# The last steps of an attention block: where PE transposes the normalised rows and VectorE takes their extremes

## The chip, the cores and the metric

The kernel runs on one core of one Trainium2 chip. The metric is the device time of the program in microseconds, from one launch. The engines are named as in the profile: PE is TensorE, DVE is VectorE, ACT is ScalarE, POOL is GpSimd, and SP is the engine whose queue issues all the DMAs here.

## The reference, cut to what matters

Eight batches of 128 rows of 512 pass through cross attention (32 query heads of 128, 4 heads of keys and values, 256 keys from the context and from the rows themselves) and through a feed-forward block whose activations are quantised by their largest and smallest value over all batches.

```python
x = x + xattn(_layernorm(x), ctx_4096, Wq, Wk, Wv, Wo)
x = x + ffn(_layernorm(x), w_gate, w_up, w_down)

def act_qdq(x, bits=16):                 # used on the input of the ffn first
    mn = jnp.minimum(jnp.min(x), 0.0)    # over the whole tensor
    mx = jnp.maximum(jnp.max(x), 0.0)
    scale = jnp.maximum((mx - mn) / qmax, 1e-12)
    ...
```

So between the two halves stands a layer norm of every batch and an extreme over all eight.

## The kernel before, in words

Attention is cut into 64 steps (`STEPS`), 16 for each of the four key heads (`QUADS`): step t takes batch `t % 16 // 2` and four of the eight query heads of that key head. The last 16 steps, 48 to 63, finish the batches, two steps for each. All operands are split in two fp16 parts, a high one written by ACT and a low one by DVE.

Each engine runs one loop over t with its own list written out by hand; engines meet at semaphores alone, and each works strictly in its order.

- PE (from line 463): `scores(t + 2)`, `project(t - 1)` (the heads times Wo, into `y`), `q_first(t + 6)`, `head_out(t)` (probabilities times values), `q_second(t + 6)`. There is no more q after step 57, and no more scores after step 61. In steps 60 to 63 `transpose_x2(b)` turns the rows of batches 0 to 6 into banks for the feed-forward block, four transposes a batch, by the table `X2_AT`; before the change it stands ahead of `project(t - 1)`. It waits for the rows (`ln2_out`) and, from batch 2, for the copy of the batch two before (`x2_copied`).
- ACT: `p_upper(t + 1)`, `exps(t + 2)`, `copy_x2(b)` by the same table, the high part of the head's output (`o_hi`), `q_upper(t + 6)`. `exps` waits for `maxima` (`max_out`).
- DVE: `maxima(t + 2)`, `p_lower(t + 1)`, work on the feed-forward weights (`unit_scales`, `unit_round`, `unit_lo`), in even steps `add_y(t - 1)`, `reciprocals(t + 2)`, in even steps from 50 `ln2_stats(b)`, the low part of the head's output (`o_lo`), `q_lower(t + 6)`, and in even steps from 50 `ln2_apply(b)`, with b = `t % 16 // 2 - 1`. `ln2_apply` waits for the root from POOL (`ln2_rstd`), writes the normalised rows (`xln2`), then takes the largest and smallest of each row of `y` (`y_extremes`) and scales them into `stats`.
- POOL: `unit_normalise`, `unit_dequantise`, `normalise(t + 2)` (four operations, one for each head, waiting for the reciprocals), and in even steps from 50 `ln2_root(b)`.
- SP: `turn_p(t + 1)`, a DMA that transposes the probabilities of the next step as soon as `p_lower` has written them, and around it the loads and stores of weights; in steps 49 to 59 also two transposing loads of ready weights after each turn (line 263).

After the loop come the last projection, 12 matmuls that only keep PE busy, the transposes of batch 7, and a short chain of small operations that gives the quantiser of the feed-forward input; then ACT and DVE round the input and PE starts on the gate.

Lines in the profile: 413 is `scores`, 423 `head_out`, 437 and 441 `project`, 450 `transpose_x2`, 323 the q matmuls (a helper), 499 gate and up, 350 the warming matmuls; 798 and 801 are `maxima`, 809 `reciprocals`, 852 the rows, 837, 838 and 857 the extremes and their statistic, 842 to 846 `ln2_stats`, 864 `add_y`; 743 is every low part (with 1024 columns it is `p_lower`), 558 every high part (with 1024 columns `p_upper`), 600 the exps, 611 `copy_x2`; 1112 is `normalise`, 1136 and 1142 are units, 1146 is `ln2_root`; 259 is `turn_p`.

Of the kernel before, what the change touches and what calls it, by code (L numbers as in the profile page):

```python
# [19 lines left out]
B, T, H = 8, 128, 512  # L20
# [6 lines left out]
QUADS = 16  # L27
# [23 lines left out]
P_FIRST = 8  # L51
OQ_PIECES = [(0, 0, 2), (0, 2, 5), (0, 5, FT)] + [(b, *span) for b in range(1, B) for span in ((0, 5), (5, FT))]
X2_AT = {60: (0, 1), 61: (2, 3), 62: (4, 5), 63: (6,)}
EARLY = 4
SLOT_OF = (5, 9, 13, 25)
WO_AT = (1, 2, 3, 4, 5, 6, 13, 14)
# [3 lines left out]
def units_at(t, stage):  # L60

    n = t - stage
    return (EARLY + n // 2,) if n >= 0 and n % 2 == 0 and EARLY + n // 2 < UNITS else ()

# [19 lines left out]
def build(nc, x, ctx_t, wq, wk, wv, wo, w_units, w_ready, out):  # L84
    stack = ExitStack()
    with stack:
# [11 lines left out]
        def sem(name):  # L98
            return stack.enter_context(nc.semaphore(name))
# [102 lines left out]
        ln2_stat, ln2_mv, ln2_var, ln2_rstd, ln2_out = (sem(n) for n in ("ln2_stat", "ln2_mv", "ln2_var", "ln2_rstd", "ln2_out"))  # L202
# [114 lines left out]
        def _(pe):  # L317
# [63 lines left out]
            def q_head(f, i):  # L381

                h, pair = 2 * (f % 4) + i, f % QUADS // 4
                return three(banks[QB + f % 2][:, i * 256:i * 256 + 256],
                             lambda r, c: wq_s[:, r, c, h * D:(h + 1) * D],
                             lambda r, c: src_t[:, 5, r, c, pair * 256:(pair + 1) * 256], HC)
# [9 lines left out]
            def q_second(f):  # L396

                q_head(f, 1).then_inc(q_mm, 1)
# [28 lines left out]
            def project(t):  # L427

                par, hq = t // QUADS % 2, t % 2
                if t % QUADS == 0:  # L430
                    pe.wait_ge(wo_lo, t // QUADS * GH + GH)
                if hq == 0 and t >= 2:
                    pe.wait_ge(y_add, t // 2)
                pe.wait_ge(o_hi, t + 1)
                for hh in range(4):
                    for r in range(2):
                        nc.tensor.matmul(banks[YB][:, :], o_s[:, 0, hh * P:(hh + 1) * P], wo_s[:, par, r, hq * 4 + hh, :],  # L437
                                         start=hq == 0 and hh == 0 and r == 0, stop=False)
                pe.wait_ge(o_lo, t + 1)
                for hh in range(4):  # L440
                    mm = nc.tensor.matmul(banks[YB][:, :], o_s[:, 1, hh * P:(hh + 1) * P], wo_s[:, par, 0, hq * 4 + hh, :],  # L441
                                          start=False, stop=hq == 1 and hh == 3)
                mm.then_inc(wo_mm, 1)

            def transpose_x2(b):
                pe.wait_ge(ln2_out, b + 1)
                if b >= 2:
                    pe.wait_ge(x2_copied, b - 1)
                for c in range(HC):
                    mm = nc.tensor.transpose(banks[QB + b % 2][:, c * P:(c + 1) * P], xln2[:, b, c * P:(c + 1) * P], ident[:, :])  # L450
                mm.then_inc(x2_mm, 1)
# [19 lines left out]
            for t in range(STEPS):  # L471
                f = t + Q_AHEAD
                if t + AHEAD < STEPS:
                    scores(t + AHEAD)
                for b in X2_AT.get(t, ()):
                    transpose_x2(b)
                if t >= 1:
                    project(t - 1)
                if f < STEPS:
                    q_first(f)  # L480
                head_out(t)
                if f < STEPS:
                    q_second(f)
            project(STEPS - 1)
            keep_warm(12)
            transpose_x2(B - 1)
# [69 lines left out]
        def _(act):  # L556
            def hi(dst, src, scale):
                return nc.scalar.activation(dst, src, ACT.Copy, scale=scale)  # L558
# [29 lines left out]
            def q_upper(f):  # L588
                act.wait_ge(q_mm, f + 1)
                head = 2 * (f % 4)  # L590
                hi(q_s[:, f // 4 % 2, 0, head:head + 2, :], banks[QB + f % 2][:, :].rearrange("p (h t) -> p h t", h=2),
                   PROJ_OUT).then_inc(q_hi, 1)
# [16 lines left out]
            def copy_x2(b):  # L609
                act.wait_ge(x2_mm, b + 1)  # L610
                nc.scalar.activation(x2t[:, :, b * P:(b + 1) * P], banks[QB + b % 2][:, :].rearrange("p (c t) -> p c t", c=HC),
                                     ACT.Copy, scale=1.0).then_inc(x2_copied, 1)
# [40 lines left out]
            for t in range(STEPS):  # L653
                f = t + Q_AHEAD
                if t + 1 < STEPS:
                    p_upper(t + 1)
                for v in units_at(t, 2):
                    unit_hi(v)
                for n in wo_at(t):
                    wo_upper(n)  # L660
                if t + AHEAD < STEPS:
                    exps(t + AHEAD)
                for b in X2_AT.get(t, ()):
                    copy_x2(b)
                act.wait_ge(pv_mm, t + 1)
                if t >= 1:
                    act.wait_ge(wo_mm, t)
                hi(o_s[:, 0, :], banks[OB][:, :], HEAD_OUT).then_inc(o_hi, 1)
                if f < STEPS:
                    q_upper(f)  # L670
            copy_x2(B - 1)

            def rounded(dst, src, q):
# [66 lines left out]
        def _(dve):  # L740
# [62 lines left out]
            def p_lower(t):  # L803
                dve.wait_ge(p_hi, t + 1)
                lo(p_16[:, t % 2, 1, :], p_s[:, t % 2].rearrange("p c h t -> p (c h t)"), p_16[:, t % 2, 0, :], 1.0).then_inc(p_lo, 1)
# [30 lines left out]
            def y_extremes(b):  # L836
                nc.vector.tensor_reduce(y_ext[:, b, 0:1], y[:, b, :], AX.X, ALU.max)
                nc.vector.tensor_reduce(y_ext[:, b, 1:2], y[:, b, :], AX.X, ALU.min).then_inc(y_ext_out, 1)

            def ln2_stats(b):  # L840
                dve.wait_ge(y_add, (NG - 1) * B + b + 1)
                nc.vector.bn_stats(bn[:, b, :], y[:, b, :]).then_inc(ln2_stat, 1)
                dve.wait_ge(ln2_stat, b + 1)
                nc.vector.bn_aggr(mv[:, b, :], bn[:, b, :]).then_inc(ln2_mv, 1)
                dve.wait_ge(ln2_mv, b + 1)
                nc.vector.tensor_scalar(veps[:, b:b + 1], mv[:, b, 1:2], 1e-5, None, ALU.add).then_inc(ln2_var, 1)
                if b == B - 1:
                    y_extremes(b)

            def ln2_apply(b):  # L850
                dve.wait_ge(ln2_rstd, b + 1)
                nc.vector.tensor_scalar(xln2[:, b, :], y[:, b, :], mv[:, b, 0:1], rstd[:, b:b + 1], ALU.subtract, ALU.mult).then_inc(ln2_out, 1)
                if b < B - 1:
                    y_extremes(b)

                dve.wait_ge(y_ext_out, b + 1)
                nc.vector.tensor_scalar(stats[:, QX, :, b], y_ext[:, b, :], mv[:, b, 0:1], rstd[:, b:b + 1],
                                        ALU.subtract, ALU.mult).then_inc(x2_stat, 1)
# [65 lines left out]
            for t in range(STEPS):  # L924
                f = t + Q_AHEAD
                final = t >= STEPS - QUADS
                if t + AHEAD < STEPS:
                    maxima(t + AHEAD)
                if t + 1 < STEPS:
                    p_lower(t + 1)  # L930
                for v in units_at(t, 0):
                    unit_scales(v)
                for v in units_at(t, 1):
                    unit_round(v)
                for v in units_at(t, 3):
                    unit_lo(v)
                for n in wo_at(t):
                    wo_lower(n)
                if t >= 2 and t % 2 == 0:
                    add_y(t - 1)  # L940
                if t + AHEAD < STEPS:
                    reciprocals(t + AHEAD)
                for n in wq_at(t):
                    wq_lower(n)
                if final and t % QUADS >= 2 and t % 2 == 0:
                    ln2_stats(t % QUADS // 2 - 1)
                dve.wait_ge(o_hi, t + 1)
                lo(o_s[:, 1, :], banks[OB][:, :], o_s[:, 0, :], HEAD_OUT).then_inc(o_lo, 1)
                if f < STEPS:
                    q_lower(f)  # L950
                if final and t % QUADS >= 2 and t % 2 == 0:
                    ln2_apply(t % QUADS // 2 - 1)
            nc.vector.memset(ones, 1.0).then_inc(ones_set, 1)
            add_y(STEPS - 1)
            ln2_stats(B - 1)
            ln2_apply(B - 1)


# [129 lines left out]
            for i in range(len(OQ_PIECES) + 4):  # L1088
                if i < len(OQ_PIECES):
                    b, first, end = OQ_PIECES[i]  # L1090
# [127 lines left out]
```

## Time and profile before

| what | value |
|---|---|
| time, median of 3 runs | 842.85 us (842.85, 842.87, 840.63) |
| time of the profiled execution | 840.5 us, its span 838.7 us |
| mean granted TensorE clock | 0.979 |
| PE busy | 780.6 us, 93% |
| DVE busy | 600.7 us, 72% |
| ACT busy | 435.4 us, 52% |
| POOL busy | 229.7 us, 27% |

The span runs from the first to the last instruction; all times of rows are microseconds from its start. Attention ends at about 615 us. The shares are means over stages with different limits, so that what an edit in steps 50 to 63 is worth has to be read in their own stretch.

### The profile page before, as it was taken

Reading aid. Unit: us, or ns where it says so; the run is one execution under the profiler, and the core shown is the slowest. Engines: PE = TensorE matmul, PEld = TensorE weight load, DVE = VectorE, ACT = ScalarE, POOL = GpSimd, SP = SyncE. Lnnn points to the kernel's source line nnn. Section 1 sums busy time; section 2 is a strip of 40 time slices with the busy share of each in tenths; the row PEclk is TensorE's granted clock in tenths of the full one; section 3 lists DMA queues with packets and bytes.
Section 4 is the critical chain, followed back from the end, with each engine's and each line's share of the span. In section 5 each row is a group of like instructions: output and inputs, shape, how many; then the busy total and the mean of one; then the engine's idle time right before and its main releaser. Section 6 shows DMA issues by size and latency. Waiting matters only on the chain.

```text
span 838.7 us, 12575 instructions
## 1 busy us (share of the span) xinstructions
PE 780.6 (93%) x4747; PEld 464.9 (55%) x4747; DVE 600.7 (72%) x1110; ACT 435.4 (52%) x946; POOL 229.7 (27%) x366
## 2 busy tenths in 40 slices
PE   8998999999999999999999999998779999931998
PEld 3455566666666666666666666665334444410443
DVE  5874558778767778767778768998746459979431
ACT  6253456655656655655655655554532019763910
POOL 0210303456443355443356343442200000000000
PEclk9999999999999999999999999999999999975999
DMA  9221055866555666455666446987651000000010
GB/s 320 69 76 51 15 144 114 181 141 137 114 127 117 172 150 132 110 126 125 164 151 141 102 99 138 170 179 137 128 109 35 1 0 1 1 1 0 26 38 38
DMA packets 203436, 85.49 MB, mean 102 GB/s; under 512 B 170352, under 2 KB 186736, under 8 KB 203376
## 3 DMA queue, kind: packets, MB, share of 16 engines
q1 hardware_dynamic: 203376, 84.69, 44.1%
q8 instruction: 37, 0.61, 0.3%
q14 instruction: 23, 0.19, 0.1%
HBM read 31.72 MB, written 10.75 MB: 51 GB/s over the span
## 4 chain that ended last, share of the span: by engine, by line
PE 78%; DVE 9%; DMA 3%; POOL 3%; ACT 3%; issue 3%; SPq 1%; ACTq 0%; POOLq 0%; DVEq 0%
PE bank L323 22%; PE bank L499 14%; PE bank L437 11%; PE bank L413 8%; PE bank L423 8%; PE bank L550 7%; PE bank L441 6%; POOL arena L1112 2%; DMA arena<-in_x 2%; DVE arena L743 2%; ACT arena L675 1%; DVE arena L1073 1%; DMA arena<-in_w_units 1%; ACT arena L600 1%; DVE nraw L798 1%
## 5 line engine op out<-in xcount | busy, mean ns | idle before, releaser
L323 PE MATMUL bank<-arena 128*128 128x256 f16 (+1 forms) x1872 | 261.0, 292 | 4.9 <-DVE arena L743 3.4
L323 PEld LDWEIGHTS bank<-arena 128*128 128x128 f16 x1872 | 182.8, 98 | 87.0 <-DVE arena L743 5.4
L1112 POOL TENSOR_SCALAR arena<-arena,rsum 128x256 f32<-128x256 f32 x256 | 132.7, 518 | 311.6 <-DVE rsum L809 297.4
L743 DVE SCALAR_TENSOR_TENSOR arena<-bank,arena 128x512 f16<-128x512 f32 x168 | 114.6, 688 | 118.1 <-ACT arena L558 117.9
L743 DVE SCALAR_TENSOR_TENSOR arena<-arena 128x512 f16<-128x512 f32 (+5 forms) x196 | 171.0, 885 | 26.4 <-ACT arena L558 26.4
L558 ACT ACTIVATE arena<-bank 128x512 f16<-128x512 f32 x168 | 98.7, 598 | 168.1 <-PE bank L423 92.5
L558 ACT ACTIVATE arena<-arena 128x512 f16<-128x512 f32 (+6 forms) x172 | 135.2, 809 | 43.5 <-POOL arena L1112 18.6
L600 ACT ACTIVATE arena<-bank,nmax 128x256 f32<-128x256 f32 x256 | 117.6, 471 | 60.5 <-DVE nmax L801 60.5
L437 PE MATMUL bank<-arena 128*128 128x512 f16 x512 | 121.0, 379 | 1.3 <-ACT arena L558 1.2
L499 PE MATMUL bank<-arena 128*128 128x512 f16 x528 | 115.8, 383 | 2.1 <-DVE arena L743 2.1
L413 PE MATMUL bank<-arena 128*128 128x256 f16 x768 | 94.3, 273 | 2.8 <-DVE arena L743 2.8
L423 PE MATMUL bank<-arena 128*128 128x512 f16 x384 | 93.4, 379 | 3.0 <-DMA arena<-arena 3.0
L499 PEld LDWEIGHTS bank<-arena 128*128 128x128 f16 x528 | 52.0, 99 | 65.9 <-issue 4.8
L413 PEld LDWEIGHTS bank<-arena 128*128 128x128 f16 x768 | 75.0, 98 | 12.7 <-DVE arena L743 3.4
L798 DVE TENSOR_REDUCE nraw<-bank 128x4 f32<-128x1024 f32 x64 | 78.3, 1223 | 3.2 <-PE bank L413 3.2
L437 PEld LDWEIGHTS bank<-arena 128*128 128x128 f16 x512 | 49.8, 98 | 49.0 <-ACT arena L558 1.5
L675 ACT ACTIVATE arena<-arena,qc 128x1024 int32<-128x1024 f32 (+5 forms) x58 | 60.4, 1080 | 28.3 <-DVE qc L981 28.3
L441 PE MATMUL bank<-arena 128*128 128x512 f16 x256 | 65.7, 379 | 0.0
L423 PEld LDWEIGHTS bank<-arena 128*128 128x128 f16 x384 | 37.2, 98 | 36.9 <-DMA arena<-arena 4.9
L550 PE MATMUL bank<-arena 128*128 128x512 f16 x264 | 57.1, 379 | 0.0
L600 ACT ACTIVATION_READ_ACCUMULATOR arena<-bank,nmax 128x1 f32 x256 | 51.8, 202 | 0.0
L1013 DVE TENSOR_SCALAR_CACHE_REDUCE arena<-bank 128x512 f32<-128x512 f32 x44 | 30.2, 687 | 26.1 <-PE bank L499 26.0
(93 smaller groups left out, 482.6 us busy)
## 6 DMA issues: line engine op xcount, KB each, us to landing
arena<-in_w_units SPq DMA_DIRECT2D x33, 256.0 KB, 3.6
w_ready<-arena SPq DMA_DIRECT2D x33, 256.0 KB, 3.3
arena<-in_wq SPq DMA_DIRECT2D x32, 256.0 KB, 3.5
arena<-in_wo SPq DMA_DIRECT2D x32, 256.0 KB, 3.6
arena<-in_x SPq DMA_DIRECT2D x1, 2048.0 KB, 15.3
out<-arena SPq DMA_DIRECT2D x8, 256.0 KB, 2.0
arena<-in_wk SPq DMA_DIRECT2D x4, 256.0 KB, 4.6
arena<-in_ctx_t SPq DMA_DIRECT2D x4, 256.0 KB, 5.0
```

What stands on the lines that cost most here:

```text
L323: last = nc.tensor.matmul(bank, a(i, c), b(j, c), start=start and c == 0 and n == 0, stop=stop and c == chunks - 1 and n == 2)
L413: mm = nc.tensor.matmul(o, q_s[:, buf, i, h, (b % 2) * P:(b % 2) * P + P], kv5[:, g + 1, r, :, b * P:(b + 1) * P], start=n == 0, stop=n == 2)
L423: mm = nc.tensor.matmul(banks[OB][:, :], kv[:, g + 1, 2 + i, (c * B + b) * P:(c * B + b + 1) * P], pt_s[:, t % 2, r, c, :], start=c == 0 a ...
L437: nc.tensor.matmul(banks[YB][:, :], o_s[:, 0, hh * P:(hh + 1) * P], wo_s[:, par, r, hq * 4 + hh, :], start=hq == 0 and hh == 0 and r == 0, ...
L441: mm = nc.tensor.matmul(banks[YB][:, :], o_s[:, 1, hh * P:(hh + 1) * P], wo_s[:, par, 0, hq * 4 + hh, :], start=False, stop=hq == 1 and hh ...
L499: mm = nc.tensor.matmul(banks[bank][:, :], wgu[:, m * FT + t, i, c * P:(c + 1) * P], xq[:, j, c, th * 512:(th + 1) * 512], start=c == 0 an ...
L550: mm = nc.tensor.matmul(banks[b % 4][:, :], oq[:, h, t, b * P:(b + 1) * P], wd_s[:, t, r, :], start=t == 0 and m == 0, stop=t == FT - 1 an ...
L558: return nc.scalar.activation(dst, src, ACT.Copy, scale=scale)
L600: nc.scalar.activation(p_s[:, t % 2, :, hh, :], bank[:, (hh % 2) * 256:(hh % 2) * 256 + 256].rearrange("p (c t) -> p c t", c=2), ACT.Exp, ...
L743: return nc.vector.scalar_tensor_tensor(out=dst, in0=src, scalar=scale, in1=part, op0=ALU.mult, op1=ALU.subtract)
L798: nc.vector.tensor_reduce(nraw[:, :], psum[:, s:s + 2, :].rearrange("p b (h t) -> p (b h) t", h=2), AX.X, ALU.max, negate=True).then_inc(n ...
L1112: done = nc.gpsimd.tensor_scalar(p_s[:, t % 2, :, hh, :], p_s[:, t % 2, :, hh, :], rsum[:, t % 2, hh:hh + 1], P_SCALE, ALU.mult, ALU.mult)
```

## The change

Four edits. On PE `transpose_x2` moves from between `scores` and `project` to the end of the step; on ACT `copy_x2` moves from ahead of the head's copy to the end of the step. On DVE the normalised rows of batch b move from the end of an even step to the next odd step, behind `p_lower` (steps 51, 53, ..., 63). The extremes are taken out of `ln2_apply` and `ln2_stats` into `ln2_extremes`, and follow the table `EXT_AT`: batches 0 to 3 at the end of that same odd step, batches 4, 5 and 6 at the end of steps 61, 62 and 63. After the loop batch 7's extremes and statistic come ahead of its rows.

```diff
+EXT_AT = {51: 0, 53: 1, 55: 2, 57: 3, 61: 4, 62: 5, 63: 6}
...
@@ PE, the loop over steps
                 if t + AHEAD < STEPS:
                     scores(t + AHEAD)
-                for b in X2_AT.get(t, ()):
-                    transpose_x2(b)
                 if t >= 1:
                     project(t - 1)
...
                 if f < STEPS:
                     q_second(f)
+                for b in X2_AT.get(t, ()):
+                    transpose_x2(b)
@@ ACT, the loop over steps
                     exps(t + AHEAD)
-                for b in X2_AT.get(t, ()):
-                    copy_x2(b)
                 act.wait_ge(pv_mm, t + 1)
...
                 if f < STEPS:
                     q_upper(f)
+                for b in X2_AT.get(t, ()):
+                    copy_x2(b)
@@ DVE, ln2_stats, ln2_apply
-                if b == B - 1:
-                    y_extremes(b)

             def ln2_apply(b):
                 dve.wait_ge(ln2_rstd, b + 1)
                 nc.vector.tensor_scalar(xln2[:, b, :], y[:, b, :], mv[:, b, 0:1], rstd[:, b:b + 1], ALU.subtract, ALU.mult).then_inc(ln2_out, 1)
-                if b < B - 1:
-                    y_extremes(b)
-
+
+            def ln2_extremes(b):
+                y_extremes(b)
+                dve.wait_ge(ln2_rstd, b + 1)
                 dve.wait_ge(y_ext_out, b + 1)
                 nc.vector.tensor_scalar(stats[:, QX, :, b], y_ext[:, b, :], mv[:, b, 0:1], rstd[:, b:b + 1],
                                         ALU.subtract, ALU.mult).then_inc(x2_stat, 1)
@@ DVE, the loop over steps
                 if t + 1 < STEPS:
                     p_lower(t + 1)
+                if final and t % QUADS >= 3 and t % 2 == 1:
+                    ln2_apply(t % QUADS // 2 - 1)
...
                     q_lower(f)
-                if final and t % QUADS >= 2 and t % 2 == 0:
-                    ln2_apply(t % QUADS // 2 - 1)
+                if t in EXT_AT:
+                    ln2_extremes(EXT_AT[t])
             nc.vector.memset(ones, 1.0).then_inc(ones_set, 1)
             add_y(STEPS - 1)
             ln2_stats(B - 1)
+            ln2_extremes(B - 1)
             ln2_apply(B - 1)
```

## Rows read from the trace of the kernel before

**Rows 1.** The page's slices of the span, busy tenths of PE.

```profile
PE   8998999999999999999999999998779999931998
```

**Rows 2.** Stretches of the span: its us, busy us and instructions of each engine, clock, DMA.

```profile
548.00:574.00 26.00, 26.00 (x178) 17.14 (x176) 24.43 (x41) 12.55 (x34) 9.88 (x17) 1.00 0.78 152
...
587.00:601.00 14.00, 10.51 (x60) 5.53 (x57) 9.86 (x18) 8.34 (x24) 4.51 (x10) 1.00 0.71 134
```

**Rows 3.** Waits of PE from 480 to 626 us: us in total, times, longest.

```profile
PE bank L450 <- DVE arena L852: 3.1, 2, 2.2
PE bank L423 <- DMA arena<-arena: 3.0, 3, 1.9
PE bank L450 <- ACT arena L611: 2.8, 1, 2.8
```

**Rows 4.** Timeline of PE: start, us, engine, line, what [idle before, releaser].

```profile
570.44 1.47 PE L413 MATMUL bank<-arena 128*128 128x256 f16 x12
...
582.89 1.47 PE L423 MATMUL bank<-arena 128*128 128x512 f16 x6 [1.91 <-DMA arena<-arena]
...
591.38 1.47 PE L413 MATMUL bank<-arena 128*128 128x256 f16 x12
592.70 1.04 PE L450 MATMUL bank<-ident,arena 128*128 128x128 f32 x8
593.57 1.89 PE L437 MATMUL bank<-arena 128*128 128x512 f16 x8
...
596.31 1.47 PE L423 MATMUL bank<-arena 128*128 128x512 f16 x6
600.62 1.11 PE L450 MATMUL bank<-ident,arena 128*128 128x128 f32 x8 [2.84 <-ACT arena L611]
...
613.01 1.90 PE L437 MATMUL bank<-arena 128*128 128x512 f16 x8 [0.69 <-ACT arena L558]
...
625.94 1.51 PE L499 MATMUL bank<-arena 128*128 128x512 f16 x4 [2.08 <-DVE arena L743]
```

**Rows 5.** Timeline of DVE, in steps 58 to 62.

```profile
572.90 1.21 DVE L798 TENSOR_REDUCE nraw<-bank 128x4 f32<-128x1024 f32 x1
...
575.12 1.23 DVE L743 SCALAR_TENSOR_TENSOR arena<-arena 128x1024 f16<-128x1024 f32 x1
...
582.68 1.22 DVE L798 TENSOR_REDUCE nraw<-bank 128x4 f32<-128x1024 f32 x1
...
594.58 0.55 DVE L852 TENSOR_SCALAR arena<-arena,mv,rstd 128x512 f32<-128x512 f32 x1 [0.92 <-POOL rstd L1146]
...
596.34 0.29 DVE L857 TENSOR_SCALAR stats<-y_ext,mv,rstd 128x2 f32<-128x2 f32 x1
596.54 1.22 DVE L798 TENSOR_REDUCE nraw<-bank 128x4 f32<-128x1024 f32 x1
...
601.48 0.69 DVE L743 SCALAR_TENSOR_TENSOR arena<-bank,arena 128x512 f16<-128x512 f32 x1 [1.28 <-ACT arena L558]
603.55 1.23 DVE L743 SCALAR_TENSOR_TENSOR arena<-arena 128x1024 f16<-128x1024 f32 x1 [1.38 <-ACT arena L558]
```

**Rows 6.** Timeline of POOL and of ACT, in steps 60 to 62.

```profile
591.78 2.13 POOL L1112 TENSOR_SCALAR arena<-arena,rsum 128x256 f32<-128x256 f32 x4 [3.21 <-DVE rsum L809]
593.99 0.55 POOL L1146 TENSOR_TENSOR rstd<-veps,mhalf 128x1 f32<-128x1 f32 x1
...
598.05 0.47 ACT L600 ACTIVATE arena<-bank,nmax 128x256 f32<-128x256 f32 x1 [3.05 <-DVE nmax L801]
...
602.46 1.06 ACT L558 ACTIVATE arena<-arena 128x1024 f16<-128x1024 f32 x1 [1.01 <-POOL arena L1112]
```

**Rows 7.** The turning DMA of line 259: all 64, then the one issued at 576.4.

```profile
DMA to landing us min/median/max: 4.2/4.3/6.5
...
DMA to landing us min/median/max: 6.5/6.5/6.5
```

**Rows 8.** The line of the rows: duration in ns, least, median, most.

```profile
L852 DVE TENSOR_SCALAR arena<-arena,mv,rstd x8: 539/626/1261, 517.2 to 618.7; 128x512 f32<-128x512 f32 x8
```

## The prediction

> **What bounds the kernel now.** I read the page's slices first: TensorE stands at 9 from slice 5 to slice 27, and then 8, 7, 7 follow, 566 to 629 us, where attention ends [rows 1]. The change touches steps 50 to 63 only (some 508 to 615 us), so the next view is the stretch table: from 548 to 574 us PE is busy for all 26.00 us with DVE at 24.43, and from 587 to 601 PE has only 10.51 of 14.00 [rows 2]. The list of waits says on what: DMA (the turned P) for 3.0 us, the normalised rows for 3.1, a copy of transposed rows for 2.8 [rows 3]. None of these waits lies before step 58. So steps 51 to 57 are bound by PE and can't gain; steps 58 to 63 are bound by a chain, and it is that chain which I re-time.
>
> The timelines show it. I write scores(n), maxima(n) and so on for step n's tile. One tile goes scores, maxima (DVE), four exps (ACT), reciprocal (DVE), normalise (POOL), p_upper (ACT), p_lower (DVE), turn (DMA), head_out (PE). In the last steps DVE is where it lies still: scores(63) is issued at 591.38 and over by about 592.8 [rows 4], yet maxima(63) begins only at 596.54, since DVE stands in ln2_apply(5): its rows wait until 594.58 for the root that POOL makes at 593.99, behind normalise(62) from 591.78 [rows 5, 6]. Then come 0.55 us of rows and, until 596.5, the extremes with their statistic. p_lower(63) follows at 603.55. The same happens to maxima(61), begun at 582.68.
>
> **The change part by part.** No instruction is added or dropped; each is moved.
>
> *Extremes, 1.5 us for a batch* (from the end of the rows at 595.1 to the 0.29 us statistic and maxima at 596.54 [rows 5]). For batches 0 to 3 they go from the end of an even step to the end of the next odd one, where they stand before the maxima of an even step. Batches 4, 5, 6 go to the ends of steps 61, 62, 63, where no maxima follow (the last, of tile 63, is at the head of step 61). There they lie beside PE's work and cost nothing; without that cover each is 1.5 us.
>
> *Rows, 0.55 us* (1.26 beside a POOL operation, below). They go to the next odd step, behind p_lower and ahead of the reciprocals. p_lower already needed the normalising that stands ahead of the root on POOL, so the wait for the root is gone. Queued behind them now are the reciprocals and so POOL: 0.55 us later in odd steps, a term that I count.
>
> *Transposes and copies.* Eight transposes take 0.87 us of PE (592.70 to 593.57 [rows 4]) at either place. What goes is the wait in front of them, 2.8 and 2.2 us [rows 3], since PE runs projection and head first. On ACT the head's copy no longer stands behind two copies. SP's queue keeps its order, as do POOL's instructions.
>
> Now the walk, which starts where PE still sets the pace. PE's last q matmul ends as scores(60) starts, 570.44 [rows 4]; ACT's and DVE's parts of it take 0.6 and 0.7, so DVE is free at 571.8. Extremes(3) follow, and maxima(60) starts at 573.3, against 572.90 [rows 5]: 0.4 **later**. p_lower(59) still ends a little earlier, 575.9 against 576.35, since maxima(60) then took 2.2 us to its successor and I allow the usual 1.3 (nmax 0.17 behind 1.14). Exps(60) run until 576.9, normalise(60) until 579.4, p_upper(60) until 580.4. DVE does the statistics of batch 4 and the head's low part until 578.7, then maxima(61) at once: **4.0 earlier** than 582.68. Exps(61) 580.4 to 582.3; p_lower(60) ends 581.6.
>
> A turned P took 4.2 us from issue to landing at least, 4.3 in the median, and 6.5 at most, that of tile 59 just behind two weight loads [rows 7]. These bound tiles 59 to 61; I take 4.3 to 6.5 for 59, some 5.3 for 60 and 61, 4.2 for 62 and 63, when no loads are left. Tile 59 lands at 580.2 to 582.4 (head_out(59) was at 582.89 [rows 4]). Scores(62) and project(59) follow by 586 to 587.5, head_out(60) at 587.0, the moved transposes until 589.3, scores(63) 589.3 to 590.7.
>
> On DVE maxima(62) lies at 583.6, p_lower(61) at 586.2 to 587.4, behind p_upper(61). Now maxima(63) starts with its scores' end, 590.8: **5.7 earlier** than 596.54. ACT: exps(63) 592.4 to 594.3; POOL: normalise(63) 594.7 to 596.9 (four operations in 2.13 us [rows 6]); p_upper 1.06; p_lower(63) 597.9 to 599.2 against 603.55 to 604.8; its turn lands at 603.4.
>
> PE from there, 2.7 us for a projection, 1.3 for a head [rows 4]: project(60) 590.6, head_out(61) 593.2, transposes until 595.4, project(61) until 598.0, head_out(62), transposes until 600.3, project(62) until 602.8, head_out(63) at 603.4, its copy, **project(63) at 605.6**. It was 613.01 [rows 4]: 7.4 earlier. With 6.5 for tile 59 and for tile 60, PE reaches project(63) at 606.8, 6.2 earlier. I take between them, 6.9. After the loop, batch 7's rows now follow its statistic: 0.29 us later for the last transposes, which hold PE ahead of the transpose of the worst values. That gives 0.3 back. Nothing else in the rest of the kernel changes; the weights of the down projection are loaded that much earlier too.
>
> **Sum:** 6.9 − 0.3 = 6.6 us less. The profiled execution took 840.5 us (span 838.7), so it would be 833.9. The three runs had 842.85 in the median, two of them at that value and one at 840.63, near the profile's; on the median the sum gives 836.2.
>
> *A shared port.* The same rows instruction took 539 ns at least and 1261 at most [rows 8]; the long ones start beside a POOL operation on a whole unit. The Trainium skill says why ("SBUF — State Buffer", section "SBUF: two separate sides"): VectorE in its two-port mode and GpSimd hold one pair of ports by an exclusive lock, and the loser "fully blocks". The trace agrees. By that rule the move is a risk, since rows now precede the reciprocals. As a mechanism of this kernel: rows of batches 4, 5 and 6 each meeting POOL's normalising cost 0.7 more apiece, 2.1 in all, and 838.3 would come out. In my walk POOL's work is over when each of them starts (579.9 and 591.7 against 581.6 and 593.3), so I don't add it.
>
> **Rivals.**
> 1. *The turned P becomes the wait.* For it: tile 59 needed 6.5 us [rows 7], and head_out already waits 3.0 [rows 3]. Against: the weight loads end with step 59. If every turn takes 6.5, head_out(63) waits until 605.7 on top of 0.6 from the earlier ones: project(63) at 608.5, 4.5 earlier, less 0.3: 838.6. The port rule's 838.3 falls beside it.
> 2. *The gain stops at another wait, or the move doesn't do what it says*: DVE isn't what holds the chain, only PE's own waits at transposes (2.8 and 2.2) are swapped for equal ones at head_out. Against it is the row: maxima(63) starts the moment the statistic is done, 3.7 us after its scores [rows 4, 5]. The time would be 842.9, at best 840.4.
> 3. *Slower: DVE becomes the bound in steps 51 to 57.* Rows and extremes now lie in the same odd step, 2.1 us of work, 2.8 with a blocked port, and DVE has just 1.6 us free in 26 [rows 2]. If all of it lands on PE's path in each of four odd steps, 11.2 us are lost against 6.6 won: 847.4. It decides from 2.3 us per odd step (2.5 net beyond the gain). Against: as much work leaves the even step, which is the fuller one (unit scales, y, statistics lie there), and the wait for the root, 0.6 to 1.3 us of DVE per pair, goes too.
> 4. *More*: steps 59 to 61 turn in 4.2 us and maxima(60) isn't pushed: 8.5 to 10 us, 833 to 834.5.
>
> **How the numbers follow.** Chances: the forecast's own case (5 to 8.5 us less, 834.4 to 837.9) 0.67; rival 1 with the port (2.6 to 5 less) 0.15; rival 4 0.08; rival 2 0.06; rival 3 0.04. A change of 0.3%, 2.5 us, is about what a measurement of this kernel tells from none. Faster 0.90, the same 0.06, slower 0.04. The range goes from rival 4's 832.5, allowing for runs near 840.6 before, to 839.9, which takes in rival 1; it leaves out rivals 2 and 3 and the ends of the rest.
>
> **What would show it.** After: maxima(61) and maxima(63) directly behind their scores; no wait of PE at a transpose inside the loop; what is left of PE's waits at head_out, on the DMA; project(63) 6 to 7.5 us earlier; steps 51 to 57 without a wait of PE. Wrong if PE shows idle time before step 58 (rival 3), if turns in steps 61 to 63 take over 5 us (rival 1), or if the stretch from the last projection to the first gate matmul, 12.9 us now [rows 4], grows by over a microsecond.

## The result and the profile after

The changed kernel takes **836.51 us** in the median of 5 runs (835.15 to 837.26); the kernel before took 841.54 us beside it (5 runs, 840.57 to 842.87). The ratio is 0.9934, its 95% interval 0.992 to 0.9947: 5.5 us less by the ratio, 5.0 by the medians. 836.2 was forecast. The profiled execution took 836.62 us (span 834.8) against 840.5 (838.7): 3.9 less. The forecast's steps are read in it.

The list of PE's waits from 480 to 626 us answers to [rows 3]:

```profile
PE bank L424 <- DMA arena<-arena: 3.9, 2, 2.0
PE bank L500 <- DVE arena L744: 2.1, 1, 2.1
PE bank L451 <- DVE arena L851: 1.4, 1, 1.4
PE bank L493 <- DVE x_worst L1000: 0.7, 1, 0.7
PE bank L438 <- ACT arena L559: 0.4, 1, 0.4
```

Lines have moved by one to three: 424 is `head_out`, 438 `project`, 451 `transpose_x2`, 260 `turn_p`. No wait at a transpose is left inside the loop (the 1.4 us is batch 7's, behind it, 1.0 before). What is left is one cause, the turned P: two waits of 1.9 and 2.0 us. The timeline of PE answers to [rows 4]:

```profile
582.27 1.47 PE L424 MATMUL bank<-arena 128*128 128x512 f16 x6 [1.91 <-DMA arena<-arena]
...
589.64 1.47 PE L414 MATMUL bank<-arena 128*128 128x256 f16 x12
...
600.54 1.89 PE L438 MATMUL bank<-arena 128*128 128x512 f16 x8
602.26 1.03 PE L442 MATMUL bank<-arena 128*128 128x512 f16 x4
605.31 2.62 PE L424 MATMUL bank<-arena 128*128 128x512 f16 x6 [2.02 <-DMA arena<-arena]
607.73 1.06 PE L451 MATMUL bank<-ident,arena 128*128 128x128 f32 x4
608.62 2.01 PE L438 MATMUL bank<-arena 128*128 128x512 f16 x8
...
622.05 3.56 PE L500 MATMUL bank<-arena 128*128 128x512 f16 x9 [2.08 <-DVE arena L744]
```

Up to project(62), which ends at 603.3, PE keeps to the forecast within 0.6 us. Then head_out(63) waits 2.02 us and lasts 2.62 us instead of 1.47. project(63) starts at 608.62, 4.4 us earlier than before and not 6.9. The timeline of DVE answers to [rows 5]: maxima(60), (61) and (63), and the end of batch 7.

```profile
573.53 1.22 DVE L799 TENSOR_REDUCE nraw<-bank 128x4 f32<-128x1024 f32 x1
...
578.69 1.21 DVE L799 TENSOR_REDUCE nraw<-bank 128x4 f32<-128x1024 f32 x1
...
591.15 1.23 DVE L799 TENSOR_REDUCE nraw<-bank 128x4 f32<-128x1024 f32 x1 [0.82 <-PE bank L414]
...
613.87 0.68 DVE L839 TENSOR_REDUCE y_ext<-arena 128x1 f32<-128x512 f32 x1
614.65 0.29 DVE L857 TENSOR_SCALAR stats<-y_ext,mv,rstd 128x2 f32<-128x2 f32 x1
614.85 0.54 DVE L851 TENSOR_SCALAR arena<-arena,mv,rstd 128x512 f32<-128x512 f32 x1
```

maxima(63) now waits for its scores (the releaser is PE), where before the finished scores lay waiting for DVE: it starts 5.4 us earlier. The eight rows operations (line 851) took 0.53 to 0.54 us each, none beside a POOL operation on a whole unit; before, the four of steps 50 to 56 took 0.70 to 1.26 us beside one. At the end the statistic stands alone behind the extremes: it starts 0.78 us after line 839 and holds the rows back.

The last profile view is that of the turned P. For tile 59 (issued at 576.1) and tile 63 (issued at 599.4) these are the time from issue to landing, then the packets of each DMA queue in the window from issue to landing (packets, MB, time as a share of 16 engines):

```profile
DMA to landing us min/median/max: 6.1/6.1/6.1
DMA to landing us min/median/max: 5.8/5.8/5.8
```

```profile
q1 hardware_dynamic: 2890, 0.73, 86.1%
q8 instruction: 1, 0.02, 1.0%
...
q1 hardware_dynamic: 2080, 0.52, 48.5%
q8 instruction: 1, 0.02, 1.0%
```

Both turns have a load of instructions beside them, one packet of queue 8; it begins at 580.2 and at 603.1. Before, tile 63's turn took 4.2 us, the least of [rows 7]: its 2080 packets were through by 608.6 and queue 8's load began at 608.9. In the changed kernel some 50 of the 2080 hadn't begun when the load did. These are the DMA packets of the changed kernel from 603.5 to 604.0 and from 604.0 to 604.5, the last ones of the turn:

```profile
DMA packets 0, 0.00 MB, mean 0 GB/s; under 512 B 0, under 2 KB 0, under 8 KB 0
...
q1 hardware_dynamic: 17, 0.00, 8.1%
```

And the clock that TensorE was granted, by stretches (1.00 is the upper of its two levels, and the lower is half of it): PE's idle time ahead of head_out(63), and the stretch behind it, with 0.53 in the mean.

```profile
603.30:605.30 2.00, 0.00 (x0) 0.00 (x0) 0.47 (x2) 0.00 (x0) 0.00 (x0) 1.00 0.02 2
605.30:607.70 2.40, 2.39 (x6) 0.95 (x7) 0.00 (x0) 0.00 (x0) 0.00 (x0) 0.53 0.00 0
```

A second stretch at the lower level lies at the first matmuls of the gate, behind PE's last wait of 2.08 us: 0.58 from 625.9 to 630.0 before, 0.57 from 622.0 to 626.0 in the changed kernel. It is the same in both, but not in every run below.

### The profile page after: what moved, and what is told of

Its sections match the earlier page's. It is cut to its first block, busy times and chain, and to the rows that moved or that the text cites. A ratio compares the mean times of both kernels' runs of the same rounds, so it can differ in the third digit from the quotient of the medians.

```text
span 834.8 us, 12583 instructions
## 1 busy us (share of the span) xinstructions
PE 781.2 (94%) x4747; PEld 466.0 (56%) x4747; DVE 596.8 (71%) x1110; ACT 436.7 (52%) x946; POOL 230.1 (28%) x366
## 4 chain that ended last, share of the span: by engine, by line
PE 84%; DVE 6%; DMA 4%; ACT 2%; issue 2%; POOL 1%; SPq 1%; DVEq 0%; ACTq 0%; POOLq 0%
PE bank L324 24%; PE bank L500 14%; PE bank L438 12%; PE bank L424 10%; PE bank L414 10%; PE bank L551 7%; PE bank L442 6%; DMA arena<-in_x 2%; DMA arena<-arena 1%; ACT arena L676 1%; DVE arena L744 1%; DVE arena L1076 1%; POOL arena L1115 1%; PE bank L351 1%; ACT arena L559 1%
```

## The experiments

Every ratio is to runs of the kernel before on the same chip in the same batch, with a 95% interval. In the same measure the changed kernel has 0.9934 (0.992 to 0.9947).

**One half alone: PE and ACT.** On the kernel before, with DVE untouched:

```diff
                     scores(t + AHEAD)
-                for b in X2_AT.get(t, ()):
-                    transpose_x2(b)
...
                     q_second(f)
+                for b in X2_AT.get(t, ()):
+                    transpose_x2(b)
@@
                     exps(t + AHEAD)
-                for b in X2_AT.get(t, ()):
-                    copy_x2(b)
...
                     q_upper(f)
+                for b in X2_AT.get(t, ()):
+                    copy_x2(b)
```

> The kernel before with one half of the change: transposes and their copies at the end of a step, DVE untouched. Theory A (DVE's order holds the chain): maxima(63) still start some 3.5 us after scores(63), p_lower(63) ends near 604.8, its turn lands near 609, project(63) starts near 611 against 613.0: 1.9 us less than before, 839 to 840. Rival B (the two waits at transposes, 2.8 and 2.2 us, were the whole loss): project(63) near 608.6 and the time of the changed kernel, some 836.5.

Measured: 840.45 us (11 runs), ratio 0.9984 (0.9976 to 0.9993), 1.3 us less; 839 to 840 was expected. Its maxima(63) start at 597.49. PE no longer waits at transposes 0 to 5; it waits in front of project(61):

```profile
601.47 2.68 PE L437 MATMUL bank<-arena 128*128 128x512 f16 x8 [1.96 <-ACT arena L558]
```

ACT's copy of the head stands behind exps(63), and these behind the late maxima: the wait was handed on, not removed. Theory A holds, rival B falls. project(63) starts at 612.73, only 0.3 earlier than before and not the 1.9 I gave, since project(61) also ran on a lowered clock behind that wait (2.68 us for eight matmuls).

**The other half alone: DVE.** The changed kernel with `transpose_x2` and `copy_x2` back in their old places.

```diff
                     scores(t + AHEAD)
+                for b in X2_AT.get(t, ()):
+                    transpose_x2(b)
...
                     q_second(f)
-                for b in X2_AT.get(t, ()):
-                    transpose_x2(b)
```

and on ACT likewise `copy_x2`, ahead of the head's copy.

> The changed kernel with its transposes and copies back ahead of project and of the head's copy; DVE as changed. Theory A: maxima(61) and maxima(63) follow their scores, but transposes of batch 6 now stand in front of project(62) and wait for rows that are made later than before (about 604), so project(63) starts near 609.2: about 0.6 us more than the changed kernel, 837 to 838.5, with one wait of PE of 3 us or more on the rows. Rival B: no gain without the transposes' move, 841 to 843.

Measured: 839.62 us (11 runs), ratio 0.9981 (0.9971 to 0.9991), 1.6 us less; 837 to 838.5 was expected. maxima(63) start at 590.90, as early as in the changed kernel. But PE comes to the transposes of batch 6 before its rows exist:

```profile
PE bank L451 <- DVE arena L851: 5.3, 2, 3.9
```

```profile
604.31 0.66 PE L451 MATMUL bank<-ident,arena 128*128 128x128 f32 x4 [3.93 <-DVE arena L851]
604.80 3.46 PE L438 MATMUL bank<-arena 128*128 128x512 f16 x8
```

The mechanism is theory A's; the size was off, 611.23 for project(63) against 609.2, for project(62) behind that wait lasted 3.46 us instead of 1.89. So the halves give 1.3 and 1.6 us, and 5.5 together. Each takes away the wait that hides the other's gain.

**Extremes directly behind the rows.** The changed kernel without the putting off:

```diff
                 if final and t % QUADS >= 3 and t % 2 == 1:
                     ln2_apply(t % QUADS // 2 - 1)
+                    ln2_extremes(t % QUADS // 2 - 1)
...
-                if t in EXT_AT:
-                    ln2_extremes(EXT_AT[t])
```

> The changed kernel with the extremes of every batch directly behind its rows in the odd step, ahead of the reciprocals. Theory A: in steps 59 and 61 the reciprocals, so POOL and the turned P, come 1.0 to 1.5 us later each; project(63) 1.2 to 2.5 us later, 837.7 to 839. Rival: DVE has room in the last steps whatever the order, time equal to the changed kernel within 0.5 us.

Measured: 835.46 us, ratio 0.9928 (0.9916 to 0.9941), not slower than the changed kernel. My expectation of 1.2 to 2.5 us more was wrong. What I had worked out did happen: the last turn was issued at 600.6 instead of 599.4. But maxima(60) came 1.3 us earlier:

```profile
572.26 1.22 DVE L799 TENSOR_REDUCE nraw<-bank 128x4 f32<-128x1024 f32 x1
```

since in step 57 DVE waits for ACT behind the reciprocals (0.91 and 0.62 us in the changed kernel), and batch 3's extremes now lie where that room is. Tile 59's turn is issued 1.0 us earlier, PE's wait for it is 1.29 us against 1.91. In the times the two sides cancel. In the trace project(63) starts at 608.05, 0.6 us earlier than in the changed kernel, but only because this execution kept the full clock at head_out(63) (1.47 us, not 2.62): at equal clock it would be some 0.6 later, an estimate from these two rows. This execution kept it at the gate too (1.00 from 621.3 to 625.3), and its part behind the gate's start is 1.2 us shorter.

**Batch 7: rows ahead of the statistic** (`ln2_statistic`, the last instruction of `ln2_extremes`, taken out of it).

```diff
-            ln2_extremes(B - 1)
-            ln2_apply(B - 1)
+            y_extremes(B - 1)
+            ln2_apply(B - 1)
+            dve.wait_ge(y_ext_out, B)
+            ln2_statistic(B - 1)
```

> The changed kernel with batch 7's rows ahead of its statistic again (its extremes still first). The stretch from project(63) to the last transposes, 6.82 us in the changed kernel's trace and 6.32 before, shrinks by 0.3 to 0.4 us, and the time with it: 0.3 to 0.4 less. Rival: the transpose of the worst values waits for the statistic instead, no difference.

Measured: 835.39 us, ratio 0.9931 (0.9915 to 0.9948); 0.4 us can't be told apart in the time. The trace shows it: from project(63) to the gate 12.93 us, the figure of [rows 4], against 13.43 in the changed kernel.

```profile
607.93 1.90 PE L438 MATMUL bank<-arena 128*128 128x512 f16 x8 [0.25 <-ACT arena L559]
...
614.25 0.66 PE L451 MATMUL bank<-ident,arena 128*128 128x128 f32 x4 [0.97 <-DVE arena L851]
...
620.86 4.44 PE L500 MATMUL bank<-arena 128*128 128x512 f16 x12 [2.08 <-DVE arena L744]
```

6.32 us lie between the first two, 6.82 in the changed kernel: 0.39 for the order and 0.12 for project(63) at a lowered clock.

**Extremes later still**, none in step 57:

```diff
-EXT_AT = {51: 0, 53: 1, 55: 2, 57: 3, 61: 4, 62: 5, 63: 6}
+EXT_AT = {51: (0,), 53: (1,), 55: (2,), 61: (3,), 62: (4, 5), 63: (6,)}
...
-                if t in EXT_AT:
-                    ln2_extremes(EXT_AT[t])
+                for b in EXT_AT.get(t, ()):
+                    ln2_extremes(b)
```

> The changed kernel with no extremes in step 57: batch 3 goes to step 61, batches 4 and 5 to step 62. Theory A: maxima(60) start at 572.0 instead of 573.5, p_lower(59) and its turn 1.0 to 1.5 us earlier, so the 1.9 us wait at head_out(59) shrinks by as much; project(63) 0.5 to 1.5 us earlier, if the turned P of tile 63 doesn't take longer. 835 to 836. Rival: what the turn gains is lost, since the part of its landing over 4.3 us is tied to a transfer that doesn't move; no difference.

Measured: 835.35 us, ratio 0.9917 (0.9904 to 0.9931). The trace has the step that was expected, PE's wait at head_out(59) halved to 0.96 us and project(63) at 606.44, 2.2 us earlier (0.8 of it since head_out(63) lost less to the clock here, 1.85 us against 2.62); in the time the intervals overlap.

```profile
580.84 1.47 PE L424 MATMUL bank<-arena 128*128 128x512 f16 x6 [0.96 <-DMA arena<-arena]
...
603.89 1.85 PE L424 MATMUL bank<-arena 128*128 128x512 f16 x6 [2.03 <-DMA arena<-arena]
```

**What makes a turn long: weight loads?**

```diff
                     load_turned(wgu[:, u], u, wg_loaded)
-                    load_turned(wgu[:, FT + u], FT + u, wu_loaded)
...
             sp.wait_ge(wo_mm, STEPS)
+            for u in range(FT):
+                load_turned(wgu[:, FT + u], FT + u, wu_loaded)
```

> The changed kernel with the turning loads of the 11 up units taken out of steps 49 to 59 and put behind the loop. Tells the two causes of the long turn of tile 59 (6.1 us from issue to landing, 4.3 in the median) apart. Weight loads: one load fewer ahead of it, the turn lands in 4.2 to 4.8 us and PE's wait at head_out(59) falls from 1.9 us to under 0.6. Instruction load (a DMA of another queue that lay in the middle of the turn, at 580.1 us): the turn still takes about 6 us and the wait stays near 1.9. Time 835 in the first case, 836.5 in the second.

Measured: 836.73 us, ratio 0.9939 (0.9927 to 0.9952), as the changed kernel. With one weight load in front of it instead of two, tile 59's turn took as long, with the instruction load inside:

```profile
DMA to landing us min/median/max: 6.2/6.2/6.2
```

```profile
q1 hardware_dynamic: 2990, 0.76, 89.8%
q8 instruction: 1, 0.02, 0.9%
```

**Or the instruction load?** Queue 8 must then be moved in time. It loads the program of an engine as this works through it; more instructions early in PE's program should bring each later load forward.

```diff
-            keep_warm(8)
+            keep_warm(2)
+            for _ in range(36):
+                nc.tensor.matmul(banks[OB][:, 0:2], warm[:, 0:P], warm[:, 0:2], start=True, stop=True)
```

> The changed kernel with six of the eight warming matmuls at the very start left out and 36 of two columns put in, 60 more instructions (loads of weights included) in PE's program, in a stretch where PE waits for the first loads. If PE's instruction loads (queue 8) are what lengthens the turns, they move by 60 of PE's instructions, to about 575 and 598 us, between the transfers: turns of tiles 59 and 63 land in 4.2 to 4.6 us instead of 6.1 and 5.8, waits at head_out fall from 3.9 us to under 1.5, time 1.5 to 3 us less. Rival (the loads of weights or the distance to the last turn do it): both turns as before, time unchanged, or worse by what the start loses.

Measured: 832.93 us, ratio 0.9894 (0.9881 to 0.9908): 3.5 us less than the changed kernel by the medians, a little more than expected. The loads begin at 572.9 and 598.1 now, and in the windows from issue to landing of tiles 59 and 63 there is no packet of queue 8. The turns took 4.6 and 4.2 us:

```profile
q1 hardware_dynamic: 2697, 0.68, 76.3%
...
q1 hardware_dynamic: 2080, 0.52, 66.1%
```

PE waits 1.6 us for turned P's instead of 3.9. Tile 63's turn, the same 2080 packets, took 4.2 us instead of 5.8. In this execution project(63) starts 2.3 us earlier than in the changed kernel (606.36). Another 1.3 us of the profiled gain lies behind the gate's start and isn't the turns': its matmuls ran at the full clock (1.00 from 619.6 to 624.0), since the stretch at the lower level fell on the warming matmuls ahead of them, behind which PE waits for DVE in any case (0.39 us instead of 2.08).

**Half the shift**, 15 such matmuls behind all eight warming ones:

```diff
             keep_warm(8)
+            for _ in range(15):
+                nc.tensor.matmul(banks[OB][:, 0:2], warm[:, 0:P], warm[:, 0:2], start=True, stop=True)
```

> The changed kernel with 15 matmuls of two columns behind the eight warming ones at the start: 30 more instructions in PE's program instead of 60. If the place of PE's instruction load is what lengthens a turn, this must NOT help as the 60 did: 30 instructions before its old place the load falls to about 577.5 and 601 us, still inside the transfers of tiles 59 and 63, so both turns take 5.3 us or more and the time stays at 835.5 to 837. If the matmuls at the start help in themselves, it gains 2 us or more.

Measured: 832.78 us, ratio 0.9903 (0.9889 to 0.9917). I missed where the loads would fall, and so the time (835.5 to 837 was expected). It became the better test: tile 59's turn was free of the load (it began at 573.9 us), tile 63's was not (602.7 us). Landing, and the queues in each window, tile 59 and then tile 63:

```profile
DMA to landing us min/median/max: 4.4/4.4/4.4
DMA to landing us min/median/max: 6.0/6.0/6.0
```

```profile
q1 hardware_dynamic: 2459, 0.62, 73.0%
...
q1 hardware_dynamic: 2080, 0.52, 46.7%
q8 instruction: 1, 0.02, 1.0%
```

PE waits 3.0 us for turned P's and project(63) starts at 606.92. The profiled execution is the slowest of the five, 834.76 us.

**Ten instructions fewer:**

```diff
-            keep_warm(8)
+            keep_warm(3)
```

> The changed kernel with three warming matmuls at the start instead of eight: 10 instructions fewer, so that each of PE's instruction loads falls later by as much. In tile 59's and tile 63's case PE would then meet the load only when it goes on after its wait, that is behind the turn: turns of 4.2 to 4.8 us, and 833 to 834 less what the colder start costs (up to 1.5 us more). If PE's load is started well ahead of the instruction at which PE stands, the loads stay inside the transfers and the time is 836 to 838.

Measured: 833.31 us, ratio 0.991 (0.9896 to 0.9924). The mirror image, though both turns were expected to be free: tile 59's has the load inside, tile 63's is free of it (it began at 604.8, behind the landing). PE waits 2.2 us for turned P's.

```profile
DMA to landing us min/median/max: 6.0/6.0/6.0
DMA to landing us min/median/max: 4.2/4.2/4.2
```

```profile
q1 hardware_dynamic: 2786, 0.71, 86.0%
q8 instruction: 1, 0.02, 1.0%
...
q1 hardware_dynamic: 2080, 0.52, 65.9%
```

**The full shift, all eight warming matmuls kept:**

```diff
             keep_warm(8)
+            for _ in range(30):
+                nc.tensor.matmul(banks[OB][:, 0:2], warm[:, 0:P], warm[:, 0:2], start=True, stop=True)
```

> The changed kernel with all eight warming matmuls kept and 30 of two columns behind them: 60 more instructions, as in the run before that replaced six of the eight and began its attention steps 1.06 us later. Instruction loads between the turns again (572 to 575 and 598 us), both turns 4.2 to 4.8 us; the start costs 0.3 us instead of 1.06, so 832 to 832.7.

Measured: 833.85 us, ratio 0.9917 (0.9904 to 0.993); turns of 4.5 and 4.2 us, and in the profiled execution PE waits 1.0 us for turned P's and starts project(63) at 605.26. That is the 605.6 of the prediction's walk. The median is 1.2 us over the end of what I expected, and 1.1 over the run with half the shift, whose trace has more waits. So the traces order these runs by the turns that are free of a load, and the medians don't (832.9 and 833.9 with both free, 832.8 and 833.3 with one): the times show that moving the loads pays, not what one turn is worth. Why isn't shown.

**Keeping the clock.** The changed kernel with eight matmuls into a free bank (1.9 us in the trace) ahead of head_out(63):

```diff
+                if t == STEPS - 1:
+                    pe.wait_ge(exp_out, 4 * (STEPS - 1))
+                    for _ in range(8):
+                        nc.tensor.matmul(banks[SC][:, :], warm[:, 0:P], warm[:, :], start=True, stop=True)
                 head_out(t)
```

> The changed kernel with eight matmuls that only keep PE busy (1.7 us) between project(62) and head_out(63), where PE stood idle for 2.0 us and was granted 0.53 of its clock behind it. If the idle time took the clock: head_out(63) back to 1.47 us from 2.62 and project(63) 1.0 to 1.3 us earlier, time 0.3 to 1 us less in the median (not each execution lost the clock). Rival: the clock fell for another reason, head_out(63) at 2.6 again in the profile. If the turn lands in 4.2 us in this execution, the eight matmuls stand in the way instead and cost up to 1.4 us.

Measured: 836.51 us, ratio 0.9939 (0.9926 to 0.9953). The turn took 5.9 us again, head_out(63) 1.47 us at the full clock, and project(63) started at 607.58, 1.0 earlier:

```profile
605.40:607.50 2.10, 1.91 (x10) 1.00 (x10) 0.00 (x0) 0.57 (x2) 0.00 (x0) 1.00 0.00 0
```

The times show none of it. The clock isn't lost in each execution: with batch 7's rows first, head_out(63) waited the same 2.02 us and kept it.

**Together.** The edits of three runs above at once: 30 small matmuls behind `keep_warm(8)`, the later `EXT_AT`, and batch 7's rows first:

> The changed kernel with three things together: 60 more instructions at the start (30 matmuls of two columns), no extremes in step 57 (batch 3 in step 61, batches 4 and 5 in step 62), batch 7's rows ahead of its statistic. The parts by themselves: about 4, 1 and 0.4 us; once the turn of tile 59 takes 4.6 us its wait is only 0.4 us, so the later extremes can give that much and no more. 831.3 to 832.3.

Measured: 832.43 us, ratio 0.99 (0.9886 to 0.9914), 4.1 us less than the changed kernel by the medians and just over the range expected. Its waits on DMA are down to one:

```profile
PE bank L453 <- DVE arena L853: 1.2, 2, 1.0
...
PE bank L426 <- DMA arena<-arena: 0.4, 1, 0.4
```

By the times it can't be told from the shift alone, but it is ahead of both kernels: its interval ends below that of the changed kernel.

## Why the prediction was right, by its own steps

- *Steps 51 to 57 gain nothing and lose nothing.* Right: no wait of PE lies there, and DVE has more room than before (22.43 us busy from 548 to 574, against the 24.43 of [rows 2]). Part of it is the port: the prediction counted the shared port as a risk of the move alone, but the rows of steps 51 to 57 have left POOL's operations on whole units and took 2.1 us together instead of 4.2. Rival 3 is out.
- *DVE's order holds the chain.* Right, by the profile (maxima(61) at 578.69, forecast 578.7; maxima(63) at 591.15, forecast 590.8) and by the two halves: with DVE as before, moving PE's and ACT's work only moves the wait. Rival 2's swap of one wait for another is what each half does by itself.
- *Extremes of batches 4 to 6 cost nothing beside PE's work.* Right, but putting them off isn't what paid: without it the time is the same. What pays of DVE's edits is the new place behind p_lower, past the wait for the root; no run moves the rows without their extremes. That batch 3's extremes push maxima(60) back was counted (573.3, measured 573.53), yet I didn't see that they could have lain in DVE's waits for ACT.
- *Tile 59's turn, 4.3 to 6.5 us.* 6.1; head_out(60) at 587.48 (forecast 587.0), scores(63) at 589.64 (589.3), p_lower(63) ended at 599.4 (599.2).
- *Tile 63's turn, 4.2 us, since "no loads are left".* **This is the term that was off.** It took 5.8 us: 1.6 more. The reason that I gave for the long turn of tile 59, the weight loads, was wrong; it is the instruction load, and that one came to tile 63 too, because with the change the two met: the load began 4.1 us after the turn's issue before, and 3.6 us after it now. Behind the longer wait the clock fell, 1.15 us more for head_out(63). Walk and measurement agree with these two: 605.6 + 1.6 + 1.15 = 608.35 against 608.62; the 6.9 of the sum stood for 606.1, between the two walks.
- *0.3 given back at the end.* 0.39, and 0.12 by the clock.
- *The sum.* 6.6 forecast; 3.9 in the profiled execution, 5.5 in the ratio. That the median, 836.5, lies 0.3 from the 836.2 forecast is in part luck: the gain forecast was 1.1 to 1.6 us too large by the times, and the median that it was taken from, 842.85, was 1.3 above the 841.54 of the five runs.
- *The signs of being wrong.* One came true. Turns of steps 61 to 63 over 5 us were to speak for rival 1, and tile 63's took 5.8; project(63) came 4.4 us earlier and not 6 to 7.5. In the trace it starts where rival 1 put it (608.5; 608.62), there by luck, since 1.15 us of it is the clock. Rival 1 named what remained, the wait for the turned P, with the wrong cause and, at 838.6, more of it than the times show. The blocked port, 2.1 us at worst, didn't appear: the rows of batches 4, 5 and 6 took 0.54 us each.

That the profiled execution gained less than the medians has a part in the choice of executions: the one profiled before, 840.5 us, is as fast as the fastest of the five runs (840.57), that of the changed kernel, 836.62, is above its median. The rest is open: the clock behind head_out(63) differs between executions, and only one of each kernel has a trace.

## What to carry to other kernels

Where a chain of short operations over four engines bounds a stretch, look first at what stands in front of the chain's next link in an in-order queue: here the wait for the root, rows and extremes that nobody needed yet took 2.9 of the 3.7 us for which finished scores lay still (593.65 to 596.54, 0.69 us before that being the head's low part). Move both sides of such a wait at once; either half alone gave under a third of what the two gave together. And when the chain holds a DMA, compare the landing times of its repetitions; an outlier that recurs at one place of the program may be the engine's own instructions being loaded, and then a few instructions more or fewer ahead of it can be worth half as much as the edit itself (2.7 to 3.7 us here, against 5.0 by the medians). The trace of the kernel before already had this outlier away from any weight load: see below.

## What the runs showed of the hardware

- **A load of instructions lengthens a transposing DMA that it overlaps.** Turns of tiles 59 and 63 with queue 8's packet inside while their own packets were still to begin: 6.0 to 6.5 us (tile 59) and 5.3 to 6.0 (tile 63). Without: 4.4 to 4.6 and 4.2. The same kernel had both cases side by side, twice, in opposite order.
- **It does so all through the loop**, where PE doesn't wait for it: of the 896 turns in the 14 traces 69 took over 5.65 us, and each of them has a load of queue 8 that begins before it lands; no turn without one took over 5.6. In the kernel before these are the turns of tiles 19, 26, 33, 40 and 59 (5.9 to 6.5 us), the first four far from the transposing weight loads of steps 49 to 59; with half the shift they are those of tiles 14, 21, 28 and 63.
- **Not each overlap does it.** In the run with PE's and ACT's half alone the load began 0.7 us before tile 63's landing, when the last of the 2080 packets were beginning, and the turn took 4.6: what counts seems to be that packets are still to begin. Why one packet holds them up isn't shown; they stood still for half a microsecond and more in the changed kernel (above), and in the run with the extremes at once some 9 GB/s were moved for about a microsecond in the middle of the transfer.
- **Instructions come in blocks over a queue of their own.** The Trainium skill ("Runtime: NRT & Kernel Launch", section "Instruction fetch mechanics") says that an engine's sequencer loads its program in blocks of 16 KiB over a DMA queue of its own, with a cost that is mostly hidden. The trace agrees on the blocks (37 packets, 0.61 MB on queue 8, 16.4 KB each) and not on the cost: moved out of one or both of these turns, it was worth 2.7 to 3.7 us by the medians.
- **The clock fell behind waits of two to four microseconds, but not behind each.** Granted 0.53 behind 2.02 us of idle time in the changed kernel, 0.59 behind 3.93 with DVE's half alone, 0.63 behind 1.96 with PE's and ACT's half (each the mean of a stretch that lies in part at the lower level, half the clock); 1.00 behind 2.02 with batch 7's rows first and behind 2.84 in the kernel before. Behind the 2.08 us ahead of the gate it was 0.58 in the kernel before and 1.00 in three runs (extremes at once, full shift with all warming matmuls, together). With 1.9 us of matmuls in the wait ahead of head_out(63) it stayed at 1.00. What decides between the two isn't shown.
